# Attention and experts in one block: shared buffers, earlier padding, scores seven units ahead

## The reference

```python
x = x + 0.5 * ffn(layernorm(x), ...)
x = x + attn(layernorm(x), ...)          # RWKV-6 recurrence
x = x + 0.5 * ffn(layernorm(x), ...)

def ffn(x):
    x = x + msa(ln1(x))                  # softmax attention, 16 heads of 8, 512 tokens a batch
    return x + moe(ln2(x))               # 8 experts, one a token (argmax of 8 logits)

def moe(x):                              # hidden width 512
    one_hot = one_hot(argmax(x @ gate_w + gate_b))
    return sum_e one_hot[e] * (gelu(x @ w1[e]) @ w2[e])
```

## Time and profile before

| | us |
|---|---|
| median of 3 runs | 1455.57 |
| lowest and highest | 1453.61, 1456.59 |
| profiled execution, its own time | 1458.89 |
| span of the profiled execution | 1456.9 |
| PE, DVE, ACT, POOL busy in it | 1232.6, 1033.9, 860.6, 573.1 |

### The profile page before, as it was taken

One profiled execution on the slowest core, in us unless ns is written; L12 is line 12 of the kernel. 1 busy time (PEld: TensorE's weight loads), 2 busy tenths in 40 slices (PEclk: granted clock), 3 DMA queues, 4 the chain that ended last, 5 costly groups with the idle time before them and its releaser, 6 DMA issues. The chain is left out here.

```text
span 1456.9 us, 35636 instructions
## 1 busy us (share of the span) xinstructions
PE 1232.6 (85%) x12512; PEld 662.6 (45%) x12513; DVE 1033.9 (71%) x1826; ACT 860.6 (59%) x1742; POOL 573.1 (39%) x877
## 2 busy tenths in 40 slices
PE   4899999999995596398888754899999999995597
PEld 2344444444443596144455442334444444443597
DVE  5888898898983132378788755888998998983132
ACT  2588778787784353444334411588778787783353
POOL 6222323332222365355676536222323332222365
PEclk8699999999997798599999955699999999997799
DMA  7033553233110332100000005031233133201332
GB/s 233 27 103 101 160 158 111 62 120 103 60 32 29 86 97 61 47 2 3 3 2 2 3 1 174 23 101 64 95 107 109 51 118 103 61 32 33 77 95 57
DMA packets 78720, 105.95 MB, mean 73 GB/s; under 512 B 12409, under 2 KB 41692, under 8 KB 78576
## 3 DMA queue, kind: packets, MB, share of 16 engines
q1 hardware_dynamic: 71792, 90.31, 20.2%
q0 software_dynamic: 5632, 12.63, 2.6%
q10 hardware_dynamic: 1152, 1.05, 0.3%
HBM read 53.57 MB, written 50.38 MB: 71 GB/s over the span
## 5 line engine op out<-in xcount | busy, mean ns | idle before, releaser
L1004 DVE TENSOR_REDUCE maxima<-ps 128x2 f32<-128x1024 f32 x512 | 616.1, 1221 | 86.1 <-PE ps L665 84.8
L946 ACT ACTIVATE probs<-ps 128x512 f32<-128x512 f32 x1024 | 550.9, 600 | 121.9 <-PE ps L673 111.5
L665 PE MATMUL ps<-k_stack,q_stack 62*128 62x512 f32 x1024 | 390.7, 474 | 35.5 <-DVE maxima L1004 22.1
L673 PE MATMUL ps<-q_stack,k_stack 64*128 64x512 f32 x1024 | 397.0, 464 | 4.1 <-ACT q_whole L882 3.4
L683 PE MATMUL ps<-probs,v_stack 128*32 128x256 f32 x4096 | 330.3, 395 | 1.0 <-ACT probs L946 0.4
L665 PEld LDWEIGHTS ps<-k_stack,q_stack 62*128 62x128 f32 x1024 | 160.2, 194 | 233.1 <-issue 136.2
L673 PEld LDWEIGHTS ps<-q_stack,k_stack 64*128 64x128 f32 x1024 | 159.3, 187 | 30.6 <-ACT q_whole L882 8.6
L683 PEld LDWEIGHTS ps<-probs,v_stack 128*32 128x32 f32 x4096 | 81.6, 108 | 167.2 <-issue 149.2
L544 POOL CAST neg_wide<-maxima 128x16 fp32r<-128x16 f32 x64 | 12.6, 196 | 283.0 <-DVE maxima L1004 283.0
L1297 DVE COPY w_now<-w 128x512 f32 x80 | 34.3, 429 | 85.0 <-issue 49.8
L1278 ACT ACTIVATE xT<-ps,ln_b,ln_w 128x128 f32<-128x128 f32 x80 | 36.6, 457 | 89.6 <-PE ps L1249 89.6
(11 more groups left out here) (208 smaller groups left out, 1696.0 us busy)
## 6 DMA issues: line engine op xcount, KB each, us to landing
q_split<-q_parts SPq DMA_DIRECT2D x32, 512.0 KB, 3.6
k_split<-k_parts SPq DMA_DIRECT2D x32, 512.0 KB, 5.3
q_stack<-q_split SPq DMA_DIRECT2D x128, 128.0 KB, 2.6
k_stack<-k_split SPq DMA_DIRECT2D x128, 128.0 KB, 2.6
xt<-sorted SPq DMA_DIRECT2D x80, 128.5 KB, 2.1
w<-in_L_ffn_w SPq DMA_DIRECT2D x16, 256.0 KB, 3.2
rows<-in_L_attn_x SPq DMA_DIRECT2D x8, 256.0 KB, 4.1
q_stack<-max_rows SPq DMA_DIRECT2D x128, 8.0 KB
```

The costliest lines, as they stand in the source:

```text
L665: mm = t.matmul(psS[:, h, :], qs[g][score_rows(h), h // 2, u * P:(u + 1) * P], ks[g][score_rows(h), h // 2, :], start=True, stop=True)
L673: t.matmul(ring("e", G, u, n), ks[G % NG][half(h), h // 2, u * P:(u + 1) * P], qs[G % NG][half(h), h // 2, :], start=True, stop=True).then ...
L946: a.activation(probs[u % 2][:, h, :], ring("e", G, u, n), ACT.Exp, scale=float(DK) ** -0.5).then_inc(e_read, 1)
L1004: v.tensor_reduce(maxima[G % 2][:, :, pair, u:u + 1], psS[:, 2 * pair:2 * pair + 2, :], AX_X, ALU.max, negate=True).then_inc(s_read, 1)
```

## The change

It has four parts, and each `ffn` has all of them.

1. `expert_phase` becomes a function `experts` that returns the five engines' code, and these stand at the end of the same block behind attention. The end of the block and of the `Phase` between the two are gone. In their place SP waits for `scattered` (all 32 tiles' rows written) and `tables_ready`, and PE for `tables_ready` and the last readers of its PSUM banks. Since both stages now hold their buffers at the same time, six of the expert stage's buffers lie in `z_all`, in its tiles 0 to 27, which belong to batches 0 to 6.
2. ACT runs one gelu on one column behind its last attention job (`gelu_table`), so that the function table is loaded there.
3. The padding rows are written by SP alone, as soon as batch 6's places are known: `pads_ready` is signalled behind `places(6)`. Since batch 7's rows are not known yet, 640 rows are written for each expert (`PAD` = 5 tiles: up to 512 rows of batch 7, and 128), and `scatter(7)` waits until they have landed (`padded`) and writes over them.
4. Scores are computed `LEAD` = 7 units ahead instead of 8.

```diff
+def experts(nc, ctx, ps, s, z_all, expert, first_row, xs, ys):
...
+    xT = [z_all[:, i, :] for i in range(2)]
+    hidT = [z_all[:, HC * (i + 1):HC * (i + 2), :] for i in range(2)]
+    w1_now = [z_all[:, HC * (i + 3):HC * (i + 4), :].rearrange("p k c -> p (k c)") for i in range(2)]
+    yt = [z_all[:, HC * 5 + i, :] for i in range(RING)]
+    before = [z_all[:, HC * 6 + i, :] for i in range(RING)]
...
+    return sync, tensor, scalar, vector, gpsimd
...
+        PAD = TPB + 1
+        expert_sync, expert_tensor, expert_scalar, expert_vector, expert_gpsimd = experts(nc, ctx, ps, s, z_all, expert, first_row, xs, ys)
...
+        LEAD = 2 * TPB - 1
...
+                sp.wait_ge(pads_ready, 1)
+                for e in range(E):
+                    row = sp.value_load(pad_row[0:1, e:e + 1], min_val=0, max_val=E * (TOK + P) - PAD * P)
+                    sp.dma_start(xs[ds(row, PAD * P), :].rearrange("(p n) c -> p n c", n=PAD),
+                                 s["padding"][:, 0:PAD, :]).then_inc(padded, 16)
...
-                sp.wait_ge(pads_ready, 1)
-                for e in range(E // 2):
-                    row = sp.value_load(pad_row[0:1, e:e + 1], min_val=0, max_val=E * (TOK + P) - P)
-                    sp.dma_start(xs[ds(row, P), :], s["padding"][:, 0, :]).then_inc(padded, 16)
-                sp.wait_ge(padded, 16 * (E // 2))
+                sp.wait_ge(scattered, 16 * NT)
+                sp.wait_ge(tables_ready, 1)
+                expert_sync(sp)
...
+                    if p == B - 1:
+                        pool.wait_ge(padded, 16 * E)
...
-                pool.wait_ge(scattered, 16 * NT)
+                expert_gpsimd(pool)
...
-                    for u in range(TPB):
+                    for u in range(TPB - i):
                         for h in range(GROUP):
                             score(i, u, h)
...
                         unit = TPB * G + u
+                        next_G, next_u = divmod(unit + LEAD, TPB)
+                        ahead = next_G <= LAST
...
-                            score(G + 2, u, 0)
+                            score(next_G, next_u, 0)
...
+                pe.wait_ge(tables_ready, 1)
+                pe.wait_ge(s_read, 2 * TPB * NG * B)
+                pe.wait_ge(h_kept, SL)
...
+                expert_tensor(pe)
...
-                act.wait_ge(pads_ready, 1)
-                for e in range(E // 2, E):
-                    row = act.value_load(pad_row[0:1, e:e + 1], min_val=0, max_val=E * (TOK + P) - P)
-                    act.dma_start(xs[ds(row, P), :], s["padding"][:, 0, :]).then_inc(act_padded, 16)
-                act.wait_ge(act_padded, 16 * (E - E // 2))
+                a.activation(gelu_table[:], s["ln2_b"][:, 0:1], ACT.Gelu_apprx_tanh)
+                expert_scalar(act)
...
                             places(b - 1)
+                            vec.wait_ge(ranks_read, b)
+                            v.tensor_copy(pad_row[:], run[b % 2][:]).then_inc(pads_ready, 1)
```

More of the change, by code:

```diff
@@ L305, in mixer_phase, with ffn_phase @@
+def ffn_phase(nc, ps, s, x_all, z_all, rows, expert, first_row, xs, ys, qd, kd, load=None):
     with Phase(nc) as ctx:
@@ L348, in mixer_phase @@
         edge, over, crossed, row_f = sb("edge", [P, NT]), sb("over", [P, SLOTS, E]), sb("crossed", [P, SLOTS]), sb("row_f", [P, SLOTS])
-        pad_row = sb("pad_row", [P, E], I32)
+        pad_row, gelu_table = sb("pad_row", [P, E], I32), sb("gelu_table", [P, 1])
         stats_made, moments_made, spread_made, scales_made = (
@@ L376, in mixer_phase @@
         ranked, ranks_read, placed, pads_ready = sem("ranked"), sem("ranks_read"), sem("placed"), sem("pads_ready")
-        scattered, padded, act_padded = sem("scattered"), sem("padded"), sem("act_padded")
-        vector_step = sem("vector_step")
+        scattered, padded = sem("scattered"), sem("padded")
+        PAD = TPB + 1
+        vector_step, tables_ready = sem("vector_step"), sem("tables_ready")
+        expert_sync, expert_tensor, expert_scalar, expert_vector, expert_gpsimd = experts(nc, ctx, ps, s, z_all, expert, first_row, xs, ys)
         psS = ps[:, 0:4, :]
@@ L802, in _ @@
                     G = NG * b + g
-                    ahead = G + 2 <= LAST
                     for u in range(TPB):
@@ L806, in _ @@
                             pe.wait_ge(rows_placed, PLACED * (G + 1))
-                            if ahead:
-                                pe.wait_ge(loaded[(G + 2) % NG], PER_LOAD * ((G + 2) // NG + 1))
                         unit = TPB * G + u
+                        next_G, next_u = divmod(unit + LEAD, TPB)
+                        ahead = next_G <= LAST
+                        if ahead and next_u == 0:
+                            pe.wait_ge(loaded[next_G % NG], PER_LOAD * (next_G // NG + 1))
                         def values(part):
@@ L827, in _ @@
                         if ahead:
-                            score(G + 2, u, 2)
+                            score(next_G, next_u, 2)
                         exponent(G, u, 2)
@@ L832, in _ @@
                         if ahead:
-                            score(G + 2, u, 3)
+                            score(next_G, next_u, 3)
                         exponent(G, u, 3)
@@ L842, in _ @@
                     job(kind, j)
+                pe.wait_ge(tables_ready, 1)
+                pe.wait_ge(s_read, 2 * TPB * NG * B)
+                pe.wait_ge(h_kept, SL)
+                pe.wait_ge(x1_ready, SL)
+                pe.wait_ge(logits_read, SL)
+                pe.wait_ge(ranks_read, SL)
+                expert_tensor(pe)
             @block.scalar
@@ L1116, in _ @@
                     low_part(1, k)
-                for G in range(2):
-                    for u in range(TPB):
-                        for pair in range(PAIRS):
-                            reduce_pair(G, u, pair)
+                for unit in range(LEAD):
+                    for pair in range(PAIRS):
+                        reduce_pair(unit // TPB, unit % TPB, pair)
                 for b, g in steps_in_order:
@@ L1124, in _ @@
                     for u in range(TPB):
-                        if G + 2 <= LAST:
+                        next_G, next_u = divmod(TPB * G + u + LEAD, TPB)
+                        if next_G <= LAST:
                             for pair in range(PAIRS):
-                                reduce_pair(G + 2, u, pair)
+                                reduce_pair(next_G, next_u, pair)
                         if b >= 2 and (g, u) == (0, 0):
@@ L1170, in _ @@
                 vec.wait_ge(halved, SL)
-                v.tensor_copy(pad_row[:], counted[:]).then_inc(pads_ready, 1)
                 done = steps.mark(v.tensor_tensor(total[:], counted[:], base[:], ALU.subtract))
@@ L1331 @@
+                v.scalar_tensor_tensor(first_row[:], c[:, 0:SLOTS], float(P), row_f[:], ALU.mult, ALU.add).then_inc(tables_ready, 1)
+                vec.wait_ge(tables_ready, 1)
+                expert_vector(vec)
 class Signal:
@@ L2004, in ffn @@
         def ffn(dst, load=None):
-            mixer_phase(nc, ps, s, x_all, z_all, rows, expert, first_row, xs, qd, kd, load)
-            expert_phase(nc, ps, s, expert, first_row, xs, dst)
+            ffn_phase(nc, ps, s, x_all, z_all, rows, expert, first_row, xs, dst, qd, kd, load)
         ffn(ys, load)
```

216 lines of the change are left out of this document (100 added, 116 removed).

## The result

The changed kernel takes **1441.44 us** (median of 4 runs, 1439.86 to 1444.91) against 1454.59 for the kernel before on the same chip. The ratio is 0.9916, 95% interval 0.99 to 0.9933, so it is faster by 13.2 us (9.7 to 14.5 by the interval). I had forecast 1435.0 within 1430 to 1446: right in sign and inside the range, but 6.4 us short. The profiled span fell by 13.8 us instead of 20.6.

The account below looks back on a forecast made before the run. The handover from attention to experts was taken as an idle hole, and the attention loop's start as delayed. 18.2 + 0 - 1.5 + 3.9 = 20.6 us off, median 1455.57 to 1435.0; range 1430 to 1446 for 8 in 10.

Parts of the forecast that it names:

- the likeliest case: The whole change working as forecast: 1435.0 us, own range 1431 to 1440, 69 in 100.
- late padding: Rival at batch 7's scatter: padding at 230 to 310 GB/s, 3 to 9 us late a stage, 1440 to 1452; 15 in 100.
- the signs that I named: Trace checks on drain, first expert turn, first `exponent`, batch 7's scatter, waits for maxima, POOL idling on padding, expert loop's period.
- Together 18.2: Attention-to-experts handover without barriers and drain: first expert turn 8.4 us earlier in the first `ffn`, 9.8 in the second.
- theory 1: Experiments' theory, not forecast: POOL's drain lasts about 83 ns per indirect DMA since its last drain, so the change moved it.
- Behind the first turn I expect the same expert stage: After the first expert turn: queues, buffers' counts and waits unchanged, so the handover's gain reaches the end.
- The landing of the scatter, 2.15: Batch 7's last scatter: seen 2.15 us after issue, read from the kernel's last indirect write; 0.5 us off either way.
- the hole: Handover from attention to experts, no engine computing: 13.4 us (first `ffn`) and 14.8 us (second) from last scatter to first turn.
- The padding, 1.5 late: Early padding ahead of batch 7's scatter: 1.2 us late in the first `ffn`, 0.3 in the second; between 0 and 6.
- The rival of the mixed rate: Padding beside a scatter runs at 176 GB/s: 35.8 us late in all, 1469 us, slower; 4 in 100.
- Seven ahead, 3.9: Attention loop's start: first `exponent` 2.36 us earlier, one more unit costs 0.4; 2.0 a stage, 3.9 in all, bounds 0 to 4.7.
- The early table, 0: First gelu of the experts: PE's products hide all but 0.08 us of the 1.28 us table load, so no gain.

Follow-up runs that it names:

- the four versions above: Kernels with scores seven units ahead, two blocks or joined, late or early padding: ratios 0.9958 and 0.9946 late, 0.9917 and 0.9907 early.
- e5: Kernel before with the early padding alone, two blocks and handover kept: 1447.55 us against 1457.03, ratio 0.9936.
- the changed kernel's second profile: Changed kernel unaltered, run again beside three other versions on one chip: 1443.04 us, ratio 0.9907 to the kernel before.
- the one added line here: Changed kernel plus a POOL drain right behind the issue of batch 7's scatter: 1434.94 us, ratio 0.985 to the kernel before.

## Why the prediction was right, and where it was wrong

The sign came out as forecast, and the lead and the table by the mechanisms given. The time missed the likeliest case's own range (1431 to 1440) by 1.4 us and fell inside the wide one for another reason than the one that made it wide: that room was for late padding, and what took it were two errors in the handover, 5.7 and 2.45 us. So its being inside is luck. Of the signs that I named, there is no drain before the first turn, the first `exponent` is at 44.65, PE doesn't wait for the maxima and the expert loop keeps its period. But the first turn is 6.0 and 6.4 us behind the last scatter instead of 5.0, batch 7's scatter starts 1.9 and 2.2 us behind its slot cast instead of within 1, and POOL does sit idle until the padding has landed.

**The handover, "Together 18.2": this step failed.** It counted the 2.68 us drain of each stage as removed. The trace of before already had two drains of different length, 2.68 us behind 32 scatters and 3.33 behind 40 outputs, and I never asked what sets a drain's length. The changed block's drain is 5.95, so 5.2 us came back by theory 1, 5.7 by the table above. "Behind the first turn I expect the same expert stage" was right for the turns (78.32 and 81.22 us from first to last, 78.86 and 80.58 before) and wrong for what follows them.

**The landing of the scatter, 2.15: mis-sized.** Issue to seen is 3.40 us in the second stage and 3.05 in the first. The row that I read belonged to a write that moved no bytes. The first turn came 6.02 and 6.41 us behind the start of the last scatter, not 5.0, 2.4 in all.

**What filled the hole.** I gave it all to part 1, with the padding's leaving taken in. By the four versions above the join takes 5.8 to 7.4 us out of the two handovers (the two drains of 2.68 and what lies around them) and puts 5.7 back at the end, so it nets 0 to 2. The early padding takes 3.0 to 4.7 out and puts nothing back. Alone in the kernel before (`e5`), where it lands in time, it gives 8.6, since 7.96 us of landing become 3.1 in the second stage and 6.5 become 2.6 in the first.

**The padding, 1.5 late: measured 2.1.** The bytes were right. By my working `padded` is there 19.0 us behind batch 6's slots (1343.7 - 1324.71); it was 18.9 (1334.21 - 1315.33). The DMA view from 1317 to 1334 us:

```profile
DMA packets 1346, 5.81 MB, mean 342 GB/s; under 512 B 192, under 2 KB 192, under 8 KB 1344
...
q1 hardware_dynamic: 1152, 5.26, 80.0%
```

The mean takes in a slow start and end. The Trainium skill (DMA: Bandwidth & Descriptors, Bandwidth) has 341 GB/s for 1 MB, from DRAM to SBUF; the trace, in the other direction, agrees as a mean, while its full slices ran at 314 to 448. The rival of the mixed rate, 176 GB/s, is refuted. What was off is when POOL needs it: not at 1344.37, where its instruction starts, but at the end of the slot cast, 1343.55 (1343.38 + 0.17). Between release and start lie some 0.8 us (1334.21 to 1335.02 above), and they come after the padding too. So by my own 1343.7 the padding was 0.15 late there and not 0.67 early. The rest of the 1.25 measured came from the other side: from batch 6's slot cast to batch 7's it took 17.45 us instead of 18.67 (1332.78 - 1315.33, 1343.38 - 1324.71), and so POOL was ready 1.2 earlier. In the first stage 0.89 was measured. That the total of 2.1 lies near my 1.5 is partly luck: in the changed kernel's second profile the scatters start 2.16 and 3.16 us behind the cast, 3.3 late in all.

**Seven ahead, 3.9: right.** 2.26 us earlier in each stage against 2.36; slack of 1.25 us where I had 1.5, and no wait of PE for the maxima. The 0.4 for the extra unit drowns in the loop's own scatter of over 3 us and is not shown.

**The early table, 0: right**, under 0.1 a stage.

**The sum.** 20.6, less 5.7 for the end, 2.45 for landing, 0.25 for scatters that take 3.89 and 4.10 instead of 3.87, 0.65 for the padding, and 0.6 more for the lead (its place holds the earlier start alone, 4.5, and not the extra unit), is 12.15, which is what the three places show. The 2.45 are 2.17 of landing and 0.3 of the first tile's load.

The end of the second stage grew by 3.06 us rather than 2.6. The drain is not the cause: 0.46 of it lie behind the drain, from whose end to the end of the span it takes 1.71 us instead of 1.25.

Open: why a scatter is seen sooner in the first stage than in the second, whether a narrow write of real rows is seen sooner than a wide one, and why the start of the second `ffn` (recurrence's end to first reduction) takes 23.95 us in the kernel before and in `e5` and 21.9 to 22.3 in all others (in the table above it is a piece of -1.8 in "all the rest").

## What to carry to other kernels

Before you count a barrier or a drain as removed, find what sets its length; if it is work done since the last one, it moves to the next barrier, and pays only where an idle engine can take it in passing, as the one added line here does (5.2 us by its place). When a duration is taken from another row, see that this row moved bytes. When several things end a wait close together, undo them alone and together: in the handover the early padding is worth 8.6 us alone in the kernel before and 3.0 to 4.7 beside the lead of seven, so no one number is its share.

## What the runs showed of the hardware

- POOL's drain takes 82 ns for each indirect DMA issued since its last drain, the long landed ones too: 2.68, 3.33, 5.95 and 6.11 us for 32, 40, 72 and 74.
- An indirect write of 128 rows of 1,028 bytes, timed alone, is seen 2.6 us after its issue in one stage and 3.3 in the other (2.9 to 4.0 behind three more of its kind in the changed kernel), 6.65 with 1 MB of other writes beside it; one whose rows are all out of bounds takes 2.1.
- An indirect DMA starts some 0.8 us after the semaphore for which its queue waits.
- One unit less of lead turned 1.25 us or more of slack into a wait of 1.43 at every group, with a granted clock of 0.93 to 0.94 in place of 0.99 along with it: 63 to 65 us a stage, for 2.3 us at the start.
